# A three-layer graph network on one core: layer 1's last four spans taken from running sums of gathered rows

## The chip, the cores and the metric

The kernel runs on one core of a Trainium2 chip. Its engines are TensorE (PE, with its weight loads shown as PEld), VectorE (DVE), ScalarE (ACT), GpSimd (POOL) and SyncE (SP, which here only starts DMAs). The metric is the device time of one execution in microseconds (us), less being better; a kernel's time is the median of its runs.

## The reference, cut to what matters

There are 6,250 nodes with 128 features and 200,000 edges, sorted by target node (`dst`). Three GRU layers with edge weights are followed by a layer norm, then by three GIN layers without weights and a second norm:

```python
for l in range(3):                              # GRU layers
    msg = (x @ weight[l])[src] * edge_weight[:, None]
    agg = segment_sum(msg, dst, num_segments=6250)
    x = gru_cell(agg, x, w_ih, w_hh, b_ih, b_hh)
x = layernorm(x0 + x)
for W, b in ((W0, b0), (W1, b1), (W2, b2)):     # GIN layers
    x = relu((x + segment_sum(x[src], dst)) @ W.T + b)
out = layernorm(x1 + x)
```

## The kernel before, in words

**Aggregation as dense matrices.** The node states lie as `xT`, feature by node, and node-major as `Y`, 49 tiles of 128 nodes. An aggregation is a matmul of all 49 tiles of Y with a strip of the adjacency matrix for some target nodes. Two matrices are needed: `adj_w` with the summed edge weights (float32, GRU layers) and `adj_h` with the edge counts (float16, GIN layers). Both are built during GRU layer 1 and stored in DRAM.

**Layer 1: 28 slots.** The target nodes are cut into 28 spans of 224 nodes, and slot t builds span t. Each node owns 64 places for edges, and two nodes share the 128 partitions. A slot has 8 batches of 14 node pairs ("windows"). For each batch DVE makes two comparisons, `hot` (which of the 49 tiles does each edge's source lie in, L2129, 700 elements) and `hot_lo` (which row of the tile, L2131, 1,792 elements), and three products of `hot` with the weights, which are split into three bfloat16 parts (L2135, 700 elements each). PE's `build_unit` (L1232) multiplies them: for each window and half, one matmul of 98 columns (counts and first weight part) and two of 49 (the other parts), 84 in a batch. ACT moves the sums out of PSUM in 6 evictions a batch (L1653), three for counts and three for weights, and SP stores the finished strips (`store_strips`).

While slot t is built, PE aggregates the span of slot t - 1 between the batches (`add_tiles`, L1239: 49 tiles of 224 columns, float32, two passes each) and runs the GRU gates of the span of slot t - 2 (`fused_rz`, `fused_ih`, L1252 to L1259), with sigmoids and tanh on ACT (L1618, L1623) and `fused_mix` and `fused_blend` on DVE (L2096 to L2110). POOL fetches the next spans' edges with indirect DMAs (`gather`, L775; `gather_near`, L757) and writes each edge's key, row and weight parts as columns that DVE's comparisons read (`make_columns`, L796 to L802). DVE's slot t + 1 waits for these columns. PE unrolls slots 0 and 1 and runs slots 2 to 27 in a loop over one slot's body. DVE waits for `s_keep`, the store of `xT` to `x_keep`, before that loop.

**Runs in layers 2 and 3.** The last 4 spans' aggregates are not made from `adj_w` there. The last 128 x 224 edges are cut into 128 lanes of 224 consecutive edges. In round i POOL gathers the source rows of the i-th edge of every lane (`fetch_rows`, L858), DVE multiplies them by the weights (L1816) and adds the sum so far if the target node is the same (L1819). Every running sum is stored in `sum_rows`. A node's aggregate is the sum at its last edge, plus that of the lane before if its edges cross a border: POOL gathers both (`fetch_ends`, L872), DVE adds them (`join_ends`) and PE turns them (`flip_runs`). The strips of `adj_w` for these spans are aggregated in layer 1 but not stored.

**The order** is written out by hand on every engine: each waits for counts of semaphores, such as `s_bmm` (units built), `s_bev` (evicted), `s_hot` (comparisons and products), `s_colv` (column steps), `s_acc` (rounds summed) and `s_fgv` (gate steps).

## Time and profile before

| | |
|---|---|
| median of 3 runs | 2909.53 us (2908.0 to 2910.0) |
| the profiled execution's own time | 2905.17 us |
| its span | 2903.3 us |
| PE busy | 2842.1 us, 98% |
| DVE, ACT, POOL busy | 1290.2, 947.2, 815.7 us |
| layer 1, slots 3 to 27 | 142.5 to 1003.4 us |

The span goes from the first to the last instruction; the execution's own time is 1.9 us longer. Busy time is summed by engine; PE's matmuls are pipelined, and their ends are modelled, so the start of one group to the start of the next gives PE's price better than the durations.

### The profile page before, as it was taken

What the parts mean: (1) busy time and instruction counts of PE and PEld (TensorE: products, weight loads), DVE (VectorE), ACT (ScalarE), POOL (GpSimd) and SP (SyncE); (2) the same over time, 40 slices, a digit from 0 to 9 for tenths busy, and PEclk for the clock granted to TensorE, in tenths of its full rate; (3) what the DMA queues carried; (4) which work ended last, traced back from release to release, by engine and by line L of the source; (5) the groups of instructions that cost most, each with busy time, mean ns of one, the idle gap of its engine ahead of it and who ended that gap; (6) DMA issues with size and microseconds to landing.
All of it is one profiled execution on the core that took longest, in us unless ns stands there. A gap on an engine that the chain in (4) does not pass through costs nothing.

```text
span 2903.3 us, 72862 instructions
## 1 busy us (share of the span) xinstructions
PE 2842.1 (98%) x29387; PEld 1888.8 (65%) x29387; DVE 1290.2 (44%) x3163; ACT 947.2 (33%) x1891; POOL 815.7 (28%) x977
## 2 busy tenths in 40 slices
PE   5899999999999999999999999999999999999998
PEld 5899999999999965555554555555555555555554
DVE  7688888888888614344422344343400010001111
ACT  6677777777777610000001011101300010001111
POOL 4233333333333215454531445543100000000000
PEclk9999999999999999999999999999999999999999
DMA  5666666666662299988996888988478768786884
GB/s 195 241 260 261 244 242 260 259 256 241 249 258 115 94 404 345 341 338 331 353 364 233 340 338 331 362 325 328 152 304 301 300 257 306 300 301 255 311 304 166
DMA packets 134137, 810.64 MB, mean 279 GB/s; under 512 B 17208, under 2 KB 27308, under 8 KB 114076
## 3 DMA queue, kind: packets, MB, share of 16 engines
q1 hardware_dynamic: 111516, 759.24, 67.5%
q0 software_dynamic: 19808, 39.54, 4.3%
q10 hardware_dynamic: 2720, 10.62, 0.9%
q8 instruction: 57, 0.93, 0.1%
q14 instruction: 36, 0.29, 0.0%
HBM read 553.01 MB, written 256.33 MB: 279 GB/s over the span
## 4 chain that ended last, share of the span: by engine, by line
PE 95%; DVE 1%; ACT 1%; another core or an unknown queue 1%; issue 1%; DMA 1%; POOL 0%; DVEq 0%; ACTq 0%; POOLq 0%
PE ps L961 30%; PE ps L1157 27%; PE ps L1239 19%; PE ps L1232 11%; PE ps L971 1%; PE ps L972 1%; PE ps L1252 1%; PE ps L1253 1%; PE ps L974 1%; PE ps L973 1%; PE ps L1136 1%; ACT ring L1653 0%; DMA x_keep<-xT 0%; PE ps L1258 0%
## 5 line engine op out<-in xcount | busy, mean ns | idle before, releaser
L961 PE MATMUL ps<-ring,Y 128*128 128x448 f32 x2352 | 888.4, 539 | 0.0
L1157 PE MATMUL ps<-ring,Y 128*128 128x448 f16 x4116 | 780.6, 352 | 0.0
L1653 ACT ACTIVATE ring<-ps 128x490 f16<-128x490 f32 (+1 forms) x1344 | 699.1, 656 | 188.6 <-PE ps L1232 184.4
L961 PEld LDWEIGHTS ps<-ring,Y 128*128 128x128 f32 x2352 | 446.4, 190 | 434.8 <-issue 434.8
L1157 PEld LDWEIGHTS ps<-ring,Y 128*128 128x128 f16 x4116 | 402.7, 98 | 373.8
L858 POOL DMA_INDIRECT ring<-y_rows,ring x448 | 430.5, 961 | 519.1 <-PE ps L961 261.3
L1239 PE MATMUL ps<-ring,Y 128*128 (+1 forms) x2744 | 571.8, 360 | 0.4 <-ACT shared L1612 0.4
L1239 PEld LDWEIGHTS ps<-ring,Y 128*128 128x128 f32 x2744 | 504.9, 190 | 8.9 <-ACT shared L1612 0.8
L1232 PEld LDWEIGHTS ps<-shared 64*128 64x128 bf16 x18816 | 325.8, 94 | 84.7 <-issue 67.0
L1232 PE MATMUL ps<-shared 64*128 64x49 bf16 (+1 forms) x18816 | 351.8, 190 | 25.3 <-DVE shared L2135 14.6
L2135 DVE TENSOR_TENSOR shared<-shared 128x700 bf16<-128x700 bf16 x672 | 324.8, 538 | 0.0
L1816 DVE TENSOR_SCALAR ring<-ring 128x128 f32<-128x128 f32 x446 | 129.9, 291 | 388.0 <-DMA ring<-y_rows,ring 224.8
L2131 DVE TENSOR_TENSOR shared<-iota_lo,shared 128x1792 bf16<-128x1792 bf16 x224 | 253.7, 1132 | 0.0
L1560 ACT ACTIVATE xT<-ps,bcur,unscale 128x448 f32 (+1 forms) x42 | 30.4, 723 | 682.1 <-PE ps L1157 682.1
L1392 ACT ACTIVATE shared<-ps 128x448 f32<-128x448 f32 x24 | 13.0, 543 | 725.5 <-PE ps L961 684.0
L1999 DVE TENSOR_REDUCE x_tops<-xT x28 | 17.4, 620 | 482.3 <-ACT xT L1560 482.3
L2129 DVE TENSOR_TENSOR shared<-iota_key,shared 128x700 bf16<-128x700 bf16 x224 | 119.9, 535 | 151.9 <-PE ps L1232 136.0
L1819 DVE SCALAR_TENSOR_TENSOR ring<-ring 128x128 f32<-128x128 f32 x446 | 157.0, 352 | 47.6 <-DVE ring L1816 0.9
L775 POOL DMA_INDIRECT shared<-in_edges,take_now x60 | 93.5, 1559 | 265.6 <-PE ps L1232 262.3
L1965 DVE TENSOR_TENSOR shared<-shared,ps 128x384 f32 (+3 forms) x14 | 8.7, 621 | 228.5 <-PE ps L1172 228.1
L732 POOL COPY weights_stage<-shared 112x128 f32<-112x128 f32 x28 | 17.9, 639 | 189.1 <-DVE shared L2058 189.1
L1733 DVE SCALAR_TENSOR_TENSOR shared<-ps,bhh,shared 128x448 f32<-128x448 f32 x28 | 19.1, 683 | 91.6 <-ACT shared L1409 81.5
(195 smaller groups left out, 1418.0 us busy)
## 6 DMA issues: line engine op xcount, KB each, us to landing
ring<-adj_w SPq DMA_DIRECT2D x72, 2688.0 KB
ring<-adj_h SPq DMA_DIRECT2D x42, 2800.0 KB, 9.5
ring<-adj_h SPq DMA_DIRECT2D x42, 2688.0 KB, 9.2
adj_w<-ring SPq DMA_DIRECT2D x48, 2016.0 KB, 11.9
adj_h<-ring SPq DMA_DIRECT2D x56, 1372.0 KB, 5.4
ring<-adj_w SPq DMA_DIRECT2D x24, 2912.0 KB
adj_w<-ring SPq DMA_DIRECT2D x48, 728.0 KB, 6.8
sum_rows<-ring SPq DMA_DIRECT2D x64, 448.0 KB
```

The costliest lines, as they stand in the source:

```text
L775: pool.indirect_dma_start(out=edges_now[:, par, d * SHARE:d * SHARE + OWN, :].bitcast(I32) .rearrange("p e k -> p (e k)"), out_offset=None ...
L858: pool.indirect_dma_start(out=run_rows[:, i % ROW_BUFS, :], out_offset=None, in_=y_rows, in_offset=bass.IndirectOffsetOnAxis(ap=run_edges[ ...
L961: mm = pe.matmul(ps[:, bank, 0:GW], Y[:, h, :], slab(s)[:, :, h - h0, :], start=(h == 0), stop=(last and h == TILES - 1))
L1157: mm = pe.matmul(ps[:, par, 0:GW], part[:, h, :], counts_slab(par, s)[:, :, h - h0, :], start=(h == 0 and part is Y_high), stop=(h == TILE ...
L1232: mm = pe.matmul(sums, hot_lo[slots, buf, w, :], rhs, start=(part == 0), stop=(part == WPARTS - 1))
L1239: mm = pe.matmul(ps[:, AGG_BANK, 0:SPAN], Y[:, h, :], strip_w[:, bass.ds(slot, 1), :, h, :].rearrange("p o b c -> p (o b) c"), start=(h == ...
L1653: act.activation(strip[:, :, c0:c0 + UNIT * WIN].rearrange("p h (d j) -> p d h j", d=WIN)[:, :, :, w0:w1], psum_unit(a)[:, :, kind, :, :]. ...
L1816: dve.tensor_scalar(run_rows[:, buf, :], run_rows[:, buf, :], weight, None, ALU.mult).then_inc(s_prod, 1)
L1819: dve.scalar_tensor_tensor(out=run_sums[:, at, :], in0=run_sums[:, (i - 1) % SUM_BUFS, :], scalar=same_node, in1=run_rows[:, buf, :], op0= ...
L2129: dve.tensor_tensor(in_pairs(hot[:, buf, :, 0, :]), every_window(iota_key, WIDE), values(par, 0, k, WIDE), ALU.is_equal).then_inc(s_hot, 1)
L2131: dve.tensor_tensor(in_pairs(hot_lo[:, buf, :, :]), every_window(iota_lo, P), values(par, 1, k, P), ALU.is_equal).then_inc(s_hot, 1)
L2135: dve.tensor_tensor(in_pairs(hot[:, buf, :, 1 + part, :]), in_pairs(hot[:, buf, :, 0, :]), values(par, 2 + part, k, WIDE), ALU.mult).then_ ...
```

## The change

- Layer 1 takes the last 4 spans from running sums too. Their 224 rounds gather rows of the input `x` itself: 2 rounds in each of the first 7 batches of 16 slots (1 to 3, 6 to 8, 11 to 13, 16 to 18, 21 to 24). POOL gathers (`fetch_batch`), ACT scales a batch later (`scale_rows`), DVE sums four batches later (`sum_batch`), SP stores after five, four rows at a time.
- The build slots come in a new order: four times four dense spans and one of the last four spans ("stretches" of five slots), then the other eight dense spans. The slots of the last four spans (4, 9, 14, 19) build counts alone: no products, 28 matmuls of 49 columns a batch, 3 evictions.
- The tiles of the dense span in front of such a slot are added half in it (24 tiles) and half in the slot behind it (25 tiles), which runs no gates. Four sets of gates thereby go to the tail behind slot 27, with `flip_run` for the four run spans; the order of the gates is `GATE_ORDER`.
- The three weight products become one instruction of 2,100 elements; `hot` and `columns` get other layouts for it, and the columns are made in 7 steps instead of 6.
- The rounds use 16 buffers, summed in place, where there were 10 for rows and 14 for sums. This holds for layers 2 and 3 too.
- DVE waits for `s_keep` at its first blend instead of ahead of the loop. `run_edges` is loaded by SP at the start. PE loops three times over a body of five slots and unrolls the rest; the other engines unroll all slots. The scratch for POOL's DMAs is set to 8192 bytes.

```diff
-ROW_BUFS = 10
-STORE = 7
+RUN_BUFS = 16
+STORE = 4
...
+FIRST_RUN = GATHERS - RUN_SPANS
+STRETCH_DENSE = 4
+STRETCH = STRETCH_DENSE + 1
+STRETCHED = RUN_SPANS * STRETCH
+ORDER = [span for r in range(RUN_SPANS) for span in (*range(STRETCH_DENSE * r, STRETCH_DENSE * (r + 1)), FIRST_RUN + r)]
+ORDER += range(STRETCH_DENSE * RUN_SPANS, FIRST_RUN)
+GATE_ORDER = [*range(FIRST_RUN - 1), *range(FIRST_RUN, GATHERS), FIRST_RUN - 1]
+RUN_SLOTS = [1, 2, 3, 6, 7, 8, 11, 12, 13, 16, 17, 18, 21, 22, 23, 24]
+RUN_BATCHES = 7
+SCALE_LAG, SUM_LAG, STORE_LAG = 1, 4, 5
+HALF_ADDED = 24
+TAIL_TILES = [0, 6, 15, 24, 33, 42, TILES]
...
+        def rounds_at(n):
+            slot, k = divmod(n, BATCHES)
+            if n < 0 or slot not in RUN_SLOTS or k >= RUN_BATCHES:
+                return range(0)
+            first = RUN_PER_BATCH * (RUN_BATCHES * RUN_SLOTS.index(slot) + k)
+            return range(first, first + RUN_PER_BATCH)
...
+            def fetch_round(turn, i):
+                if i >= RUN_BUFS:
+                    if i % STORE == 0:
+                        use, q = divmod(i // STORE - STORE_TURNS, STORE_TURNS)
+                        pool.wait_ge(s_stored[q], 16 * (STORES // STORE_TURNS * turn + use + 1))
+                    pool.wait_ge(s_acc, RUN * turn + i - RUN_BUFS + 2)
+                pool.indirect_dma_start(out=run_bufs[:, i % RUN_BUFS, :], out_offset=None, in_=y_rows if turn else x,
+                                        in_offset=bass.IndirectOffsetOnAxis(ap=run_edges[:, i, 0:1].bitcast(I32), axis=0))\
+                    .then_inc(s_row[i % RUN_BUFS], 16)
...
+            def prepare_span(t):
+                par = t % 2
+                n = BATCHES * t
+                for k in range(2):
+                    fetch_batch(n + k)
+
+                pool.wait_ge(s_key, OWN_TILES + KEY_STEPS * (t + 2))
+                pool.wait_ge(s_colp, t + 1)
+                pool.sem_inc(s_mark_pool, 1)
+                add_own(t + 1, 1 - par)
+                take_places(t + 2, par)
+                if t in (ENDS_SLOT, ENDS_SLOT + 1):
+                    first = RUN_SPANS // 2 * (t - ENDS_SLOT)
+                    fetch_ends(0, range(first, first + RUN_SPANS // 2))
+                fetch_batch(n + 2)
+                for d, k in enumerate(FETCH_AT):
+                    pool.wait_ge(s_bmm, UNITS * (BUFS + n + k))
+                    pool.sem_inc(s_mark_pool, 1)
+                    gather(par, d)
+                    fetch_batch(n + k)
+                    if d == 0:
+                        fetch_batch(n + k + 1)
+                make_columns(t + 1, 1 - par)
+                fetch_batch(n + 6)
+                near_rows(t + 3, 1 - par)
...
-            def build_unit(n, buf, a):
+            def build_unit(buf, a, weighted):
...
-                    for part in range(WPARTS):
+                    for part in range(WPARTS if weighted else 1):
...
+                    tiles = range(0 if j else HALF_ADDED, TILES if weighted else HALF_ADDED)
...
-            with pe.Fori(0, GATHERS // 2 - 1) as i:
-                with pe.Fori(0, 2) as slot:
-                    build_span(2 * i + slot + 2, slot, 2 * i + slot)
...
+            for j in range(2, STRETCH):
+                build_span(0, j)
+            with pe.Fori(1, RUN_SPANS) as r:
+                for j in range(STRETCH):
+                    build_span(r, j)
+            for j in range(GATHERS - STRETCHED):
+                build_span(RUN_SPANS, j)
...
-            add_tiles(0, 0, SH)
-            fused_gates(GATHERS - 2)
...
+            for c, n in enumerate(range(FIRST_RUN - 2, GATHERS)):
+                add_tiles(0, TAIL_TILES[c], TAIL_TILES[c + 1])
+                if n < GATHERS - 1:
+                    fused_gates(n)
...
+                if c < RUN_SPANS:
+                    flip_run(c)
...
+            def scale_rows(n):
+                for i in rounds_at(n):
+                    row = run_bufs[:, i % RUN_BUFS, :]
+                    act.wait_ge(s_row[i % RUN_BUFS], 16 * (i // RUN_BUFS + 1))
+                    act.activation(row, row, ACT.Copy, scale=run_edges[:, i, 1:2]).then_inc(s_prod if i else s_acc, 1)
...
+            def sum_row(turn, i):
+                done = RUN * turn + i
+                row, last = (run_bufs[:, j % RUN_BUFS, :] for j in (i, i - 1))
+                dve.wait_ge(s_acc, done)
+                dve.wait_ge(s_prod, done - turn)
+                dve.scalar_tensor_tensor(out=row, in0=last, scalar=run_edges[:, i, 2:3], in1=row,
+                                         op0=ALU.mult, op1=ALU.add).then_inc(s_acc, 1)
...
-                    dve.wait_ge(s_hot, HOT * n + 1)
-                    for part in range(WPARTS):
-                        dve.tensor_tensor(in_pairs(hot[:, buf, :, 1 + part, :]), in_pairs(hot[:, buf, :, 0, :]),
-                                          values(par, 2 + part, k, WIDE), ALU.mult).then_inc(s_hot, 1)
+                    if has_weights(t):
+                        dve.wait_ge(s_hot, hot_before(t, k) + 1)
+                        dve.tensor_tensor(hot[:, buf, 1:KINDS, :, :].rearrange("p k w (x t) -> p (k w) x t", t=2),
+                                          hot[:, buf, 0:1, :, :].rearrange("p k w x -> p k (w x)").to_broadcast([P, WPARTS, BATCH * WIDE]),
+                                          columns[:, par, k, 2:2 + WPARTS, :, :].rearrange("p k w (o t) -> p (k w) o t", o=1)
+                                          .to_broadcast([P, WPARTS * BATCH, WIDE // 2, 2]), ALU.mult).then_inc(s_hot, 1)
+                    sum_batch(n - SUM_LAG)
...
-            dve.wait_ge(s_keep, 16)
...
+                if n == 0:
+                    dve.wait_ge(s_keep, 16)
```

## Rows read from the trace of the kernel before

**Rows 1.** Page, the span in 40 slices, busy tenths of PE
```profile
PE   5899999999999999999999999999999999999998
```
**Rows 2.** Stretches: length, busy time by engine (instructions), PE clock, DMA share, GB/s
```profile
0.00:104.00 104.00, 67.34 (x1567) 58.76 (x1569) 68.27 (x153) 62.61 (x124) 36.38 (x75) 0.93 0.66 239
...
142.50:1003.40 860.90, 860.72 (x19626) 798.97 (x19625) 716.75 (x1469) 662.30 (x1325) 306.19 (x404) 1.00 0.58 230
1003.40:1030.50 27.10, 26.65 (x155) 26.16 (x155) 3.20 (x9) 5.32 (x13) 0.89 (x2) 1.00 0.73 303
```
**Rows 3.** Stretches: one slot (columns: PE, PEld, DVE, ACT, POOL, clock, DMA)
```profile
486.76:521.18 34.42, 34.42 (x786) 31.95 (x785) 28.89 (x60) 26.50 (x53) 12.07 (x16) 1.00 0.63 253
```
**Rows 4.** Timeline of PE in that slot: start, duration, line
```profile
488.23 0.65 PE L1252 MATMUL ps<-shared,wT 128*128 128x224 f32 x2
...
489.95 1.53 PE L1232 MATMUL ps<-shared 64*128 64x98 bf16 x84
491.41 2.92 PE L1239 MATMUL ps<-ring,Y 128*128 x14
494.16 0.54 PE L1258 MATMUL ps<-shared,wT 128*128 128x224 f32 x2
...
495.01 0.66 PE L1232 MATMUL ps<-shared 64*128 64x98 bf16 x30
```
**Rows 5.** Timeline of DVE in slot 0, one batch and the next one's start
```profile
23.80 0.53 DVE L2129 TENSOR_TENSOR shared<-iota_key,shared 128x700 bf16<-128x700 bf16 x1
...
25.24 1.38 DVE L2135 TENSOR_TENSOR shared<-shared 128x700 bf16<-128x700 bf16 x3
26.54 0.52 DVE L2129 TENSOR_TENSOR shared<-iota_key,shared 128x700 bf16<-128x700 bf16 x1
```
**Rows 6.** Waits from 0 to 150 us: total, times, longest
```profile
PE ps L1232 <- DVE shared L2135: 14.6, 3, 7.4
...
DVE shared L2129 <- DMA x_keep<-xT: 12.2, 1, 12.2
```
**Rows 7.** Stretches: the time after that wait
```profile
99.60:106.40 6.80, 3.74 (x88) 3.57 (x89) 6.40 (x16) 2.69 (x6) 0.00 (x0) 0.50 1.00 415
```
**Rows 8.** Groups and one line's instructions: nearest rows for gate steps, sums, scalings
```profile
L2099 DVE SCALAR_TENSOR_TENSOR shared<-ps,bih,shared 128x224 f32<-128x224 f32 x12 | 5.4, 451 | 0.4
...
L1819 DVE SCALAR_TENSOR_TENSOR ring<-ring 128x128 f32<-128x128 f32 x446 | 157.0, 352 | 47.6 <-DVE ring L1816 0.9
...
L1570 ACT ACTIVATE shared<-shared,averager x47: 477/480/494, 2688.3 to 2898.7; - x35, 128x128 f32<-128x128 f32 x12
```
**Rows 9.** Row gathers of layers 2 and 3: all (ns min/median/max), then the timeline
```profile
L858 POOL DMA_INDIRECT ring<-y_rows,ring x448: 938/944/1252, 1068.5 to 2008.1; - x150
...
1259.25 0.94 POOL L858 DMA_INDIRECT ring<-y_rows,ring  x1 [0.30 <-DVE ring L1819]
```
**Rows 10.** Timeline of POOL at the start and in one slot; DVE's next slot begins
```profile
13.98 1.01 POOL L775 DMA_INDIRECT shared<-in_edges,take_now  x1 [0.84 <-POOL take_now L769]
...
497.40 1.69 POOL L775 DMA_INDIRECT shared<-in_edges,take_now  x1 [2.66 <-PE ps L1232]
506.01 1.54 POOL L775 DMA_INDIRECT shared<-in_edges,take_now  x1 [6.92 <-PE ps L1232]
...
512.72 0.44 POOL L800 CAST shared<-shared 128x224 bf16<-128x224 f32 x1 [0.17 <-POOL shared L802]
...
518.45 0.52 DVE L2129 TENSOR_TENSOR shared<-iota_key,shared 128x700 bf16<-128x700 bf16 x1 [1.48 <-PE ps L1232]
```
**Rows 11.** Timeline of PE where it stops inside a unit (slots 1 and 2)
```profile
68.84 0.71 PE L1232 MATMUL ps<-shared 64*128 64x49 bf16 x33 [0.85 <-issue]
...
129.19 0.29 PE L1232 MATMUL ps<-shared 64*128 64x49 bf16 x7 [1.99 <-issue]
```
**Rows 12.** DMA queues of instructions, 0 to 142.5 us, then 142.5 to 1003.4 us (packets, MB, share)
```profile
q8 instruction: 18, 0.29, 0.8%
...
q14 instruction: 4, 0.03, 0.0%
```

531 lines of the change are left out of this document (291 added, 240 removed).

## The prediction

> **What bounds the kernel now.** I read the page's slices first, then busy time by stage, then one slot of the layer-1 stage engine by engine. TensorE (PE) is busy in almost every slice [rows 1]. The change works in the first 1030 us. From 142.5 to 1003.4 us (slots 3 to 27, 34.4 us each) PE is busy 860.7 of 860.9 us, so there a gain is what leaves PE, as long as nobody else becomes the bound [rows 2]. One slot shows how near the others are: PE 34.4, DVE 28.9, ACT 26.5, POOL 12.1 us [rows 3]. PE's prices come from its timeline [rows 4]: one batch's build 1.46 us (489.95 to 491.41), seven aggregated tiles 2.75 to the gates behind them (0.40 a tile), gates 1.72 (r, z: 488.23 to 489.95) and 0.85 (494.16 to 495.01). DVE takes 2.74 us a batch (23.80 to 26.54), 1.44 of it the two comparisons, to the products at 25.24 [rows 5]; what is left of its 28.9 is 7.0 a slot for keys, steps, leaps and gates.
>
> **The stall in front of slot 2.** DVE waits 12.2 us there for the store of x, and PE 7.4 us in one piece for DVE [rows 6]; PE's granted clock then falls to 0.50 for 6.8 us, the lower level of 1.2 GHz [rows 7], in which its 3.7 us of work would be 1.9. The wait on s_keep moves from ahead of the loop to the first blend, some 20 us into slot 2. **-9.**
>
> **Four counts-only slots and the slots behind them.** A counts slot (j = 4) builds with a third of the matmuls. No row shows that batch; a third of 1.46 is 0.49, and in no case is it above 1.46. With 24 tiles, gates, and transposes (0.5, what is left of the slot's 34.4) PE has 3.9 + 9.6 + 2.6 + 0.5 = 16.6 us. DVE has 8 x 1.44 + 7.0 + six left-over sums at 0.39 = 20.9, ACT half its evictions, about 14.3. So DVE ends it, and POOL's columns for the next slot may add half a microsecond: 21.5. The slot behind (j = 0) has a full build but 25 tiles and no gates: PE 11.7 + 10.0 + 0.5 = 22.2, ACT 24.9 (its slot without gates), DVE 8 x 2.62 + 7.0 - 2.1 (five gate operations of up to 0.45 us, [rows 8]) = 25.9. Together 47.4 instead of 68.8; DVE comes in up to 4.5 us ahead of PE and must leave with 2.6 done, which gives another 0 to 2. I take 22 for each of four pairs: **-88** (bounds -76 and -96).
>
> **Merged product.** Three products of 700 elements stand in the 1.38 us row; one of 2,100 saves the overlapping starts, 0.12 us. It is off PE's path except at j = 0, where it is in the sum. Were it to run at half the element rate it would cost some 2.3 us, see the rivals.
>
> **Tail.** From 1003.4 PE runs 27.1 us to layer 2: 49 tiles, two sets of gates, turned chunks [rows 2]. Four more sets come in (4 x 2.57 = 10.3) and four flips (1.2); these gates were left out of the j = 0 slots above. One set's chain (r, z 1.72, then seven operations of DVE and ACT at up to 0.45 as in [rows 8], with hand-overs some 6) is shorter than PE's turn of 2.57 + 0.5 + nine tiles 3.6 = 6.7, so only its first and last ends show: **+13** (up to +18 if a joined row is late).
>
> **The run rounds, on four engines.** 224 rounds go into 16 slots, 14 a slot, all inside PE-bound slots. DVE gets 14 sums of 352 ns [rows 8], 0.39 with the dependent wait, less 8 x 0.12: 28.9 + 5.5 - 1.0 = 33.4. ACT gets 14 scalings; the nearest row is L1570, the same shape at 480 ns, 0.41 in a row [rows 8]: 26.5 + 5.7 = 32.2. Both stay under 34.4, by one to two microseconds, and DVE may run a batch ahead, so a late row is caught up rather than passed on. POOL is another matter. It is busy 12.1; three gathers that start 0.9 us after what releases them (PE ends a batch at 495.01 + 1.46, the gather starts at 497.40), seven dependent steps 0.17 apart and one more column step, 0.5, make 16.5, say 17 [rows 4, 10]. Fourteen gathers come on top. In layer 2 one costs 938 to 944 ns and they follow each other every 1.25 us [rows 9]. In the build stage the edge gathers take 1.69 and 1.54 us where one took 1.01 at the start of the kernel: each of these began while DVE was in its comparisons [rows 10]. So 14 gathers are 17.5 us from below and 14 x 2.0 = 28 from above. Only those that meet a comparison or the product should be lengthened, so I take 1.5 each, 21 us, and POOL's slot is 38. Against a PE slot of 35.8 (next part) that is 2.2 late a slot. In the first slot of each of four groups it is covered, since columns were ready 5.3 us before DVE used them (512.72 + 0.44 against 518.45, [rows 10]); in the other 12 it is not: **+27** (0 to +126). Queued behind a late gather are make_columns, for which DVE's next slot waits, and ACT's scaling, behind which stand the evictions.
>
> **PE's code.** This is what I would have missed without asking what stood in front of idle PE. In slots 1 and 2 PE stops inside a unit, with nothing to wait for: 0.85 us at 68.8 and 1.99 us at 129.2 [rows 11]. Instruction transfers of 16 KB go with it: 18 of them before 142.5 us, and in the 861 us of the loop none on that queue [rows 12]. So PE stalls where it meets code for the first time while the DMA engines are full of strip stores, and a one-slot loop body stays resident. The new PE code unrolls slots 0 to 4, loops over a body of five slots three times, and unrolls eight more. 11 PE-bound slots with new code are certain; if the five-slot body doesn't stay, it is 17. I take 17 at the 1.4 us a slot that slots 1 and 2 show, four j = 0 slots at the same, and two jumps back at 2.5: 24 + 6 + 5 = **+35**. Bounds: 11 slots at 1.4, +15; each of a slot's two store bursts catching one full stall, 4 us, 17 x 4 + 16 + 5 = +89.
>
> The Trainium skill (Runtime: NRT & Kernel Launch, section Instruction fetch mechanics) says that PE's instruction memory holds 2048 instructions, is refilled in blocks of 256, and that crossing a block is mostly hidden. The first half agrees with 16 KB packets and with a resident loop; the trace disagrees with the second by 1.99 us in one crossing. By that rule the stalls would be nought and the sum 35 lower. The same section says that a taken branch to code no longer held forces a fetch, which speaks for the two jumps.
>
> **Small ones.** The first columns in one more step, place_ends (18 dependent steps) on DVE in slot 25, eight end gathers on POOL in each of slots 26 and 27: **+3** together. Seven more iotas on POOL at the start end before the first leap count arrives. Loading run_edges moves x by 1 to 2 us, ahead of its first use. In layers 2 and 3 the stores are 56 of 4 rows instead of 32 of 7 and the rows share 16 buffers; PE there waited for none of it. 0.
>
> **Sum.** -9 - 88 + 13 + 27 + 35 + 3 = -19, against the profiled execution's 2905.2 (span 2903.3), which is 4.3 below the median of the runs, 2909.5. So 2886 in its terms and **2891** in those of the median.
>
> **Rivals.**
> 1. *Code fetch costs nothing* (the page's rule, as a mechanism here: blocks arrive ahead as they seem to in layers 2 and 3, where a block lasts long). 2891 - 35 = 2856; if gathers too keep their quiet price of 1.25, POOL's slot is 34.5 and 27 more go: 2829. Against it stand two stalls in two slots.
> 2. *POOL becomes the bound of the run slots.* At 2.0 us a gather its slot is 45, 9.2 above PE's: 16 x 9.2 less 4 x 5.3 is +126 in place of +27, so 2990, slower than before. It decides from 1.6 us a gather, where 12 x 1.6 us eats the 19 gained. For it: each of the edge gathers in the build stage is at 1.54 or above. Against: these always start right at a batch's end, as DVE starts comparing; fourteen in a row will not.
> 3. *Code fetch is dear*, 4 us a slot: +54, 2945, slower. For it: the DMA engines are nearly as busy in the loop, 0.58, as in the first 104 us, 0.66 [rows 2], and strip stores recur in every slot.
> 4. *The merged product loses its rate*: DVE's run slots at 33.4 + 8 x 1.0 = 41.4, over 5 us above PE in every full slot, about +120, so 3010. Its operands keep pairs of 16-bit elements, as before.
> 5. *The work is taken out but nobody waits less*: not likely, as PE is the bound without a gap.
>
> **Chances.** Forecast 0.43, between 2865 and 2903; rival 1 0.22; rival 2 0.14; rival 3 0.14; rival 4 0.03; rest 0.04 (any of them cut down to nearly no change). Under 0.2% (5.8 us) a measurement of this kernel can't be told from no change. From these: faster 0.58, same 0.12, slower 0.30. The range takes in rival 1's first value and the full price of rival 3, and leaves out the far ends: 2842 to 2950.
>
> **What the next profile would show.** PE's slots from 142 us on no longer alike: pairs of about 21 and 26 us, the others 34.4 plus stalls. L1232's batches in counts slots near 0.5 us. Waits of PE on "issue" of some tens in number and 25 to 40 us in sum, with instruction packets in the whole of the first 900 us (some 150 more) if the body isn't resident. Gathers on POOL in layer 1 at 1.2 us each and their line's idle small; if they are at 1.6 or more, or DVE's first comparison of a slot and ACT's scaling wait for POOL or its DMA by tens of microseconds, rival 2 is the case. No 12 us wait for x_keep. PE idle in the tail of a few microseconds. What would make me wrong outright: DVE rather than PE last in the run slots, a merged product above 1.5 us, or a lower clock in the counts slots, where PE has gaps.

## The result and the profile after

The changed kernel takes **26,368.9 us** (median of 4 runs, 26,355.2 to 26,374.5), before took 2908.8 us beside it: ratio 9.07, interval 9.057 to 9.079. I had forecast 2891 us and faster. Three single executions far above their neighbours (3001.5 and 10,422.0 us of before, 8803.6 us of one layout) are left out of the times below. The page of after shows at once that this is no slower layer 1 but another program. Its slices of the 26,372.7 us span (0.66 ms each, tenths of busy time, then granted clock and GB/s):

```profile
PE   8500000000000000000000000000000000399999
DVE  7403333333333333333333333333333333200000
POOL 5303333333333333333333333333333333100000
PEclk9755555555555555555555555555555555699999
GB/s 248 299 338 15 15 15 15 15 15 15 15 15 15 15 15 15 15 15 15 15 15 15 15 15 15 15 15 15 15 15 15 15 15 15 129 260 263 253 292 254
```

For some 21 ms TensorE does nothing and 15 GB/s move. The groups between 1082 and 23,000 us say who works there:

```profile
L979 POOL DMA_INDIRECT adj_w<-w_sum,cell x1600 | 3185.7, 1991 | 14920.0 <-DVE cell L2390 12481.1 <-issue 2438.9
L979 POOL DMA_INDIRECT adj_c<-count,cell x1600 | 3181.0, 1988 | 487.8 <-issue 487.8
```

1600 turns of two scattered adds are the kernel's other branch: it builds the adjacency in blocks of 125 edges and then runs all three layers densely. Every engine takes it when `flag` is 0, and `flag` is 1 only if the counted sum is N_EDGES + RUN_SPANS*SPAN. The second part of that sum is a test of L2312, which counts the starts of the four counts-only spans that are at least RUN_BASE (171,328). Two places in VectorE's timeline of after show what reaches it (start, duration, line):

```profile
917.51 0.16 DVE L1914 SCALAR_TENSOR_TENSOR run_last<-run_from,found 112x8 f32<-112x8 f32 x1
917.71 0.31 DVE L1916 TENSOR_SCALAR run_from<-run_from 112x8 f32<-112x8 f32 x1
...
1033.97 0.15 DVE L2312 TENSOR_SCALAR_CACHE_REDUCE run_mask<-run_from 112x8 f32<-112x8 f32 x1
...
1050.29 0.15 DVE L2315 TENSOR_SCALAR flag<-ps 1x1 int32<-1x1 f32 x1 [16.17 <-PE ps L1454]
```

L1916 is the step of `place_ends` that subtracts RUN_BASE from `run_from` in place. It used to run in layer 2, behind the test; it now runs in slot 25, 116 us ahead of it. The test then compares starts that have already lost 171,328 with 171,328.

Layer 1 of this trace is still the changed layer 1. Its tail begins (first tiles behind the last slot) at 1045.28 us, against 1003.4 in [rows 2]. The stretches of after, columns as in [rows 2]:

```profile
0.00:104.00 104.00, 67.27 (x1602) 58.98 (x1602) 75.31 (x145) 65.66 (x136) 58.71 (x100) 0.85 0.67 237
104.00:980.00 876.00, 767.35 (x16815) 691.48 (x16816) 688.91 (x1229) 654.27 (x1392) 532.75 (x630) 0.95 0.65 251
980.00:1045.30 65.30, 58.77 (x1282) 53.61 (x1280) 40.26 (x65) 43.46 (x86) 34.14 (x40) 0.97 0.60 216
```

TensorE is busy 893.4 us up to the tail (67.3 + 767.4 + 58.8), where before it was 964.6. So 71 us of work did leave it, and its idle time rose from 39 to 152 us: +42 in all. The waits of TensorE from 104 to 980 us name the idle time (total, times, longest):

```profile
PE ps L1318 <- issue: 59.8, 35, 4.2
PE ps L1318 <- DVE shared L2269: 20.3, 6, 4.9
PE ps L1318 <- ACT ring L1781: 9.5, 12, 1.7
PE ps L1325 <- issue: 8.4, 8, 2.6
PE ps L1351 <- ACT shared L1727: 6.8, 4, 6.3
```

"issue" with nothing to wait for, 68 us, is the largest. In before PE had 0.2 us idle in 861 [rows 2], and its granted clock was 1.00 there; here it is 0.95.

### The profile page after: what moved, and what is told of

The parts are those of the page before. It is cut to its first block, busy times and chain, and to the rows that moved or that the text cites. A ratio compares the mean times of both kernels' runs of the same rounds, so it can differ in the third digit from the quotient of the medians.

```text
span 26372.7 us, 202033 instructions
## 1 busy us (share of the span) xinstructions
PE 4401.5 (17%) x29364; PEld 2609.4 (10%) x29364; DVE 9180.1 (35%) x49850; ACT 927.1 (4%) x1904; POOL 6992.3 (27%) x3969
## 4 chain that ended last, share of the span: by engine, by line
DVE 28%; issue 27%; DMA 23%; PE 16%; SPq 3%; POOL 3%; DVEq 0%; POOLq 0%; ACT 0%; ACTq 0%
DMA adj_c<-count,cell 22%; PE ps L1045 12%; SPq L719 3%; POOL adj_w L979 2%; DVE shared L2355 2%; DVE shared L2354 2%; PE ps L1325 1%; DVE part_i L2387 1%; DVE scal L2383 1%; DVE scal L2386 1%; DVE scal L2366 1%; DVE scal L2373 1%; DVE cell L2390 1%; DVE scal L2379 1%; DVE scal L2377 1%
## 5 line engine op out<-in xcount | busy, mean ns | idle before, releaser
L979 POOL DMA_INDIRECT adj_w<-w_sum,cell x1600 | 3185.7, 1991 | 14920.0 <-DVE cell L2390 12481.1
L1014 PE MATMUL ps<-ident,xT 128*128 128x128 f32 x147 | 28.8, 346 | 21756.1 <-DMA shared<-x_keep 21743.9
L979 POOL DMA_INDIRECT adj_c<-count,cell x1600 | 3181.0, 1988 | 487.8 <-issue 487.8
L1045 PE MATMUL ps<-ring,Y 128*128 128x448 f32 x8232 | 3107.6, 539 | 6.5 <-DVE Y L1855 6.5
L1045 PEld LDWEIGHTS ps<-ring,Y 128*128 128x128 f32 x8232 | 1563.3, 190 | 1536.9 <-issue 1536.9
L2358 DVE CUSTOM_DVE_ANT_0 shared<-shared 125x125 f32<-125x125 f32 x3200 | 927.5, 290 | 110.5
L2355 DVE SCALAR_TENSOR_TENSOR shared<-shared,dst_c 125x125 f32<-125x125 int32 x1600 | 561.5, 351 | 57.3
L1325 PE MATMUL ps<-ring,Y 128*128 128x224 f32 x2352 | 526.2, 376 | 9.1 <-issue 8.7
L2358 DVE CUSTOM_DVE_ANT_0 shared<-shared,earlier 125x125 f32<-125x125 f32 x1600 | 463.5, 290 | 55.5
L2364 DVE TENSOR_SCALAR_CACHE_REDUCE shared<-thresholds,scal 125x55 f32<-125x55 f32 x1600 | 434.7, 272 | 56.9
L2371 DVE TENSOR_SCALAR_CACHE_REDUCE shared<-thresholds,scal 125x55 f32<-125x55 f32 x1600 | 434.3, 271 | 56.9
L1325 PEld LDWEIGHTS ps<-ring,Y 128*128 128x128 f32 x2352 | 450.3, 199 | 22.4 <-issue 8.9
L2383 DVE TENSOR_SCALAR scal<-scal 125x1 f32<-125x1 f32 x1600 | 342.2, 214 | 56.9
L2386 DVE TENSOR_SCALAR scal<-scal 125x1 f32<-125x1 f32 x1600 | 341.6, 214 | 57.3
```

The source lines that it names most:

```text
L979: pool.indirect_dma_start(out=adj.rearrange("(e o) -> e o", o=1), out_offset=bass.IndirectOffsetOnAxis(ap=cell[:, 0:1], axis=0), in_=val[: ...
L1045: mm = pe.matmul(ps[:, bank, 0:GW], Y[:, h, :], slab(s)[:, :, h - h0, :], start=(h == 0), stop=(last and h == TILES - 1))
L1325: mm = pe.matmul(ps[:, AGG_BANK, 0:SPAN], Y[:, h, :], strip_w[:, strip, :, h, :], start=(h == 0), stop=(h == TILES - 1))
L2355: step(dve.scalar_tensor_tensor(out=both, in0=dst_r[:, :], scalar=dst_c[:, 0:1], in1=same, op0=ALU.is_equal, op1=ALU.mult))
L2358: step(dve.tensor_tensor_reduce(junk, both, other[:, :], 1.0, 0.0, ALU.mult, ALU.add, acc[:, :]))
L2383: step(dve.tensor_scalar(m1, major, float(ROW), keep, ALU.mult, ALU.mult))
```

## Experiments

### The branch

One constant of the changed kernel is altered, so that the test suits starts that already had RUN_BASE taken off:

```
-            dve.tensor_scalar(run_mask[:, :, :], run_from[:, :, :], float(RUN_BASE), 0.0, ALU.is_ge, ALU.add,
+            dve.tensor_scalar(run_mask[:, :, :], run_from[:, :, :], 0.0, 0.0, ALU.is_ge, ALU.add,
                               accum_out=covered[:, 1:2]).then_inc(s_found, 1)
```

> The changed kernel with one constant altered: the coverage test counts the starts of the four counts-only spans that are at or above 0 instead of at or above 171,328. Nothing is left out; the instructions and their order are those of the changed kernel. Theory A (the placing of the run ends now runs ahead of the test and has already taken 171,328 off the starts, so that the test finds none, the flag is 0 and every engine takes the other branch): the flag is 1, the branch of before is taken, and the time is that of before plus what layer 1 lost in the trace of after, where its tail starts at 1045 us against 1003 us before, plus up to 15 us for the longer tail: 2950 to 2965 us. Theory B (the flag is 0 for another reason, the sum of the found edges): nothing changes, about 26,370 us. Theory C (the branch is taken as before, and the added time is the new layer 1 and its consequences): about 26,370 us as well.

3022.6 us (3018.9 to 3028.9, 5 runs), ratio to before 1.040 (1.038 to 1.041). Theory A stands for the 23.3 ms: theories B and C said 26,370. But my number was 60 us short, and that is the second story of this case.

The other way round, before with a flag that must fail (it is compared with `N_EDGES + RUN_SPANS*SPAN - 1`, and GpSimd waits for two early copies in the other branch):

> The kernel before with the flag compared with a number one less than the one that the counted sum reaches, so that the flag is 0 and the other branch is taken (GpSimd waits there once for two early copies into sum_rows, over long before); layer 1 is built as before. Theory A (the branch alone makes the time of after): the time of after less the 42 us that its layer 1 took longer, 26,300 us within 1%. Rival (something in the changed layer 1 slows the later stages too): well under 26,000 us.

26,319.4 us, one run. Beside it the changed kernel itself took 26,428.6, 109 us more, and its tail of layer 1 began 104 us later (1106.46 against 1002.57 us). So the old layer 1 with the other branch costs what the changed kernel costs, less what layer 1 lost. The branch alone makes the 23 ms.

### Why the mended kernel is 115 us slower

The trace of the altered test has its tail of layer 1 at 1111.24 us, 66 us behind the trace of the changed kernel, with the same instructions. TensorE and GpSimd around 264 us in it (timeline; brackets: idle before, releaser):

```profile
262.88 0.89 PE L1318 MATMUL ps<-shared 64*128 64x98 bf16 x44
264.05 0.28 PE L1318 MATMUL ps<-shared 64*128 64x49 bf16 x5 [0.28 <-issue]
264.80 0.74 PE L1318 MATMUL ps<-shared 64*128 64x98 bf16 x35 [0.48 <-issue]
265.47 2.92 PE L1325 MATMUL ps<-ring,Y 128*128 128x224 f32 x14
```
```profile
262.10 0.95 POOL L890 DMA_INDIRECT run_bufs<-in_x,run_edges  x1 [0.30 <-issue]
263.36 0.94 POOL L890 DMA_INDIRECT run_bufs<-in_x,run_edges  x1 [0.30 <-issue]
```

A batch of 84 build matmuls, 1.46 us when undisturbed, is cut up by gaps of 0.25 to 0.5 us with a handful of matmuls between them. From 100 to 1000 us I counted gaps of TensorE with releaser issue ("short gaps"): here 179 of up to 0.6 us, over half of them beginning while a row gather runs, though gathers fill only a quarter of that time; in the trace of the changed kernel 7. Kernels timed together on one chip are called a sitting here; there were six, and the altered test and the changed kernel's first trace come from two of them. Two runs asked whether the gaps belong to the program or to the sitting.

> The changed kernel once more, nothing altered. In its trace the tail of layer 1 (the first multiply of L1325 that waits 0.45 us for L1727) starts at 1045 us; in the changed kernel with the altered test, whose layer 1 has the same instructions in the same order, it starts at 1111 us, with 200 more gaps of 0.25 to 0.5 us between build matmuls (releaser issue), half of them while GpSimd issues L890's row gathers. If these gaps belong to the run or the chip and not to the program, this run and the next agree with each other, at 1045 us or at 1111 us. If they belong to the program, this one has its tail at 1045 us again and the next at 1111 us. The time is about 26,370 us either way.

> The changed kernel with the altered test once more (starts counted from 0), nothing left out. If the gaps belong to the program: 3015 to 3030 us with the tail of layer 1 at about 1111 us and over 150 short gaps. If they belong to the run or the chip: anything between 2950 us with the tail at 1045 us and 3025 us.

The changed kernel again: 26,428.6 us, tail at 1106.46 us, 177 short gaps. The altered test again: 3018.0 us, tail at 1102.79 us, 177 short gaps. So the program alone doesn't decide: the same kernel shows 7 in one trace and 177 in another.

In the same sitting, the 224 row gathers are taken out (GpSimd only signals; products, sums and stores go on with zeros; edit shortened):

```
 def fetch_round(turn, i):
     ...
+    if not turn:
+        pool.sem_inc(s_gone, 1); return
     pool.indirect_dma_start(out=run_bufs[:, i % RUN_BUFS, :], ...)
```

> The changed kernel with the altered test, and without the 224 gathers of rows of x (L890, turn 0): GpSimd only signals where it issued one, run_bufs is cleared once at the start instead, and the products, sums, stores and end gathers of the rounds go on with zeros, so that four spans of layer 1 get no sums. Theory G (GpSimd's row gathers hold back TensorE's matmuls: 98 of the 175 short gaps lie under one): the short gaps go, and the time falls by 60 to 90 us, to 2930 to 2960 us. Rival H (the gaps have to do with the instructions of TensorE alone): 10 us less at most, 3010 to 3020 us, the gaps still there. Rival I (DVE's 223 sums of 0.36 us and ScalarE's 224 products set the pace, not the gathers): the time stays within 10 us too, and no gap of releaser issue changes.

2924.9 us (ratio 1.007, 1.006 to 1.009), 27 short gaps, tail at 1007.98 us. Theory G: the gathers, not the 223 sums or the 224 products, cost some 93 us there (the tail begins 95 us earlier). What in them? Plain copies of 128 neighbouring rows, same place, same bytes (edit shortened):

```
+    if not turn:
+        pool.dma_start(run_bufs[:, i % RUN_BUFS, :], x[128 * (i % 44):128 * (i % 44) + 128, :]); return
```

> The changed kernel with the altered test, where each of the 224 gathers of rows of x (L890, turn 0) is a plain copy of 128 rows that lie together in x, issued from the same place on GpSimd: the same bytes into the same buffers in the same rhythm, but the rows are not those that the edges name, so four spans get wrong sums. Without these gathers the time was 2925 us, with them 3019 to 3023 us. Theory G1 (it is the making of 128 row addresses and descriptors on GpSimd, 0.94 us per gather, that holds TensorE back): the short gaps of 0.25 to 0.5 us between build matmuls are few, as in the run without gathers (25 instead of 175), and the time is 2925 to 2950 us. Rival G2 (it is the traffic of the rows, 128 packets of 512 bytes each, wherever it comes from): over 100 short gaps, 3000 to 3025 us. Rival G3 (a plain copy on GpSimd's queue costs it as much as a gather): GpSimd's busy time per copy is again 0.9 us and more, and the gaps stay.

2934.7 us and 13 short gaps; but the next kernel of that sitting, with its gathers, had 7, so the run told nothing of them. It was repeated, with the altered test beside it:

> Once more the kernel in which each of the 224 gathers of rows of x is a plain copy of 128 rows that lie together, issued by GpSimd (four spans get wrong sums). Its first run stood on a chip on which the layout with the last seven slots in a loop took 2915 us and had no short gaps either, so it told nothing of them. If the run beside this one (the changed kernel with the altered test) shows over 150 short gaps: G1 (the making of the rows' descriptors holds TensorE back) gives 2925 to 2950 us and few gaps here; G2 (the rows' traffic does) gives 3000 to 3025 us and over 100. If the run beside it shows few gaps and about 2955 us, this one gives 2925 to 2945 us and tells nothing of them again.

> The changed kernel with the altered test, nothing left out, on the same chip as the plain copies: 3015 to 3030 us with over 150 short gaps, as in its three runs so far, or, if this is the kind of chip of the first trace of the changed kernel, 2950 to 2965 us with few.

Altered test 3033.5 us, 176 short gaps; plain copies 2952.1 us (ratio 1.015, 1.013 to 1.017), 25 short gaps. GpSimd's row for the copies from 0 to 1000 us (in the first of the two runs), and for the gathers in the next kernel:

```profile
L892 POOL DMA_DIRECT2D run_bufs<-in_x x224 | 123.3, 557 | 125.6 <-PE ps L1322 99.0 <-DMA sum_rows<-run_bufs 8.9 <-POOL shared L865 7.1
```
```profile
L890 POOL DMA_INDIRECT run_bufs<-in_x,run_edges x224 | 251.6, 1123 | 98.5 <-issue 56.0 <-PE ps L1318 20.1 <-POOL take_now L834 10.5
```

G2 and G3 fall: where the gaps occur, they go with the plain copies, though GpSimd's DMA queue moves no less (from 100 to 860 us 18.4 MB in 9,317 packets, with the gathers 16.7 MB in 8,460), and a copy takes GpSimd 0.56 us instead of 1.12. G1 is what is left, its forecast of 2950 missed by 2 us. But a gather differs from the copy in two ways that no run separates: GpSimd makes a list from 128 row numbers, and the rows lie scattered in DRAM.

The clearest look at the effect is slot 26 of a layout in which the last seven slots are one loop body (its runs follow below). There eight gathers of run ends stand back to back. Without short gaps in the sitting the slot took 34.1 us, with them 45.3, with not one packet of TensorE's instructions on queue q8 in either: this isn't code being fetched. With the gaps TensorE got through 2 to 6 matmuls at a time, and over the slot its granted clock was 0.89 (PE, POOL, then the slot's stretch):

```profile
1003.95 1.05 PE L1318 MATMUL ps<-shared 64*128 64x98 bf16 x49
1005.45 0.29 PE L1318 MATMUL ps<-shared 64*128 64x98 bf16 x6 [0.46 <-issue]
1006.21 0.32 PE L1318 MATMUL ps<-shared 64*128 64x98 bf16 x6 [0.47 <-issue]
...
1009.88 0.32 PE L1318 MATMUL ps<-shared 64*128 64x98 bf16 x5 [1.18 <-issue]
1011.35 0.31 PE L1318 MATMUL ps<-shared 64*128 64x98 bf16 x4 [1.15 <-issue]
```
```profile
1004.17 1.00 POOL L903 DMA_INDIRECT run_bufs<-sum_rows,run_ends  x1 [1.08 <-issue]
1005.47 0.93 POOL L903 DMA_INDIRECT run_bufs<-sum_rows,run_ends  x1 [0.30 <-issue]
```
```profile
995.80:1041.10 45.30, 38.80 (x788) 34.26 (x789) 27.37 (x45) 26.57 (x53) 21.93 (x25) 0.89 0.54 203
```

It also fits that the kernel before is free of the gaps (1 in the trace with the failing flag, in the sitting where both kernels with row gathers had 177): in that trace, as in [rows 10], its 50 edge gathers from 142.5 to 1000 us start behind a finished batch, and none lies over build matmuls. Of the row gathers of the layout above, 136 of 197 do.

### TensorE's code

The kernel before, with only TensorE's slot loop written out (edit shortened):

```
-with pe.Fori(0, GATHERS // 2 - 1) as i:
-    with pe.Fori(0, 2) as slot:
-        build_span(2 * i + slot + 2, slot, 2 * i + slot)
+for t in range(2, GATHERS):
+    build_span(t, t % 2, t - 2)
```

> The kernel before with TensorE's loop over slots 2 to 27 written out, 26 copies of the body for one; every instruction of the work, every wait and every other engine stay as they are. Theory of code fetch (TensorE's instructions that it has not executed lately come in by transfers that queue behind the strip stores): the trace of after has 76 us of waits with the releaser issue on the build's matmuls in layer 1, in 26 slots of new code, 16 of which only; here all 26 are new: 2909 plus 60 to 80, 2970 to 2990 us. Rival (new code costs nothing, the issue gaps of after come from elsewhere, such as the merged product or the counts-only matmuls): 2905 to 2915 us. The 1.4 us per slot of the prediction would give 2945 us.

2974.3 us, ratio 1.023 (1.021 to 1.024): +67 us for 26 slots of new code, 2.6 us a slot, and the rival (2905 to 2915) falls. From 0 to 1060 us TensorE's waits on issue are 45.0 us ahead of build matmuls and 7.2 ahead of others, against 6.2 in before:

```profile
PE ps L1232 <- issue: 45.0, 31, 3.0
```

Part of the rest is the clock behind a stall. TensorE in the trace of the altered test, where 14 tiles behind a stall take 5.49 instead of 2.92 us at a granted clock of 0.51:

```profile
1068.50 0.77 PE L1318 MATMUL ps<-shared 64*128 64x49 bf16 x22 [2.76 <-issue]
1069.20 5.49 PE L1325 MATMUL ps<-ring,Y 128*128 128x224 f32 x14
```

In the written-out kernel the granted clock over 142.5 to 1072 us is 0.99 where [rows 2] has 1.00.

The same in the mended kernel: can the stalls be taken back with loops? First, slots 1 to 3 of a stretch and the last seven slots as loops (edit shortened):

```
 with pe.Fori(1, RUN_SPANS) as r:
-    for j in range(STRETCH): build_span(r, j)
-for j in range(GATHERS - STRETCHED): build_span(RUN_SPANS, j)
+    build_span(r, 0)
+    with pe.Fori(1, STRETCH_DENSE) as j: build_span(r, j)
+    build_span(r, STRETCH_DENSE)
+build_span(RUN_SPANS, 0)
+with pe.Fori(1, GATHERS - STRETCHED) as j: build_span(RUN_SPANS, j)
```

> The changed kernel with the altered test, and with TensorE's code in loops: the slots 1 to 3 of a stretch of five are one body run three times (stretches 1 to 3), and the last seven slots are one body run seven times, so that some 1500 instructions stay in use instead of some 9000. Nothing is left out. Theory of code fetch: most of the 76 us of issue waits of layer 1 go, and the time is 50 to 70 us below the changed kernel with the altered test: 2885 to 2910 us. Rival (the issue waits only stand where TensorE would wait for VectorE or ScalarE anyway, whose busy share of the layer is 0.79 and 0.75): within 15 us of the changed kernel with the altered test.

3058.3 us, 36 us slower than without the loops: both of my theories failed. I had also counted badly, matmuls without weight loads: one weighted slot's body is some 1600 instructions of TensorE, and three kinds of slot did not stay together. Most jumps back of the short loops show as a pair of stalls, 2.0 to 2.6 and 5.2 to 6.0 us, and as many instruction packets move as before (35 from 300 to 500 us, against 31). Then only the last seven slots as a loop and the stretches written out, `for r in range(1, RUN_SPANS)`:

> The changed kernel with the altered test, with TensorE's code laid out in another way: the four stretches of five slots are written out one after another (no loop over them, so no branch back), and the last seven slots are one body run seven times. Nothing is left out. In the run with loops in every stretch each branch back cost two stalls, of 2.0 and 5.6 to 6.0 us, and in the changed kernel the branch back of the loop over stretches cost 5.8 and 2.7 us, twice; the last slots, run from one body, had no stall of releaser issue over 0.6 us outside the slots of the end gathers. Theory: 17 us less for the two branches and 1.5 to 2.5 us for each of six repeated slots, 2990 to 3000 us. Rival (stalls of TensorE's code are hidden or made up for by the waits after them): within 5 us of 3018 to 3023 us.

2915.1 us (ratio 1.0033, 1.0017 to 1.0048), far below what I expected, in a sitting without the short gaps. Whether layout or sitting did it, four kernels in one sitting were to tell:

> The changed kernel with the altered test, nothing left out, once more, now on one chip with the layout that took 2915 us. Program theory P (the 200 short gaps come from the loop over stretches, which brings TensorE's code in again and again while GpSimd gathers rows): 3015 to 3030 us, tail of layer 1 at 1103 to 1111 us, over 150 short gaps; the written-out layouts beside it have under 40. Chip theory Q (the gaps depend on the chip or the loading of the program, as the two traces of the changed kernel itself show, tail at 1045 and at 1106 us): all kernels of this call that gather rows agree, with gaps in all or in none; without them this one takes 2945 to 2965 us.

> Stretches written out, last seven slots one body run seven times (the layout that took 2915 us), nothing left out. P: 2907 to 2925 us again, under 40 short gaps. Q with the gaps on this chip: 2980 to 3000 us; Q without them: 2907 to 2925 us, and the changed kernel with the altered test beside it is 30 to 45 us slower, the price of two branches back and of six slots' new code.

> The changed kernel with the altered test and TensorE's code of all 28 slots written out, no loop at all, nothing left out. P: few short gaps, and only the stalls of new code in every slot, so 15 to 25 us above the layout with the last seven slots in a loop: 2930 to 2945 us. If the loop of the last seven slots is what matters: as the changed kernel with the altered test.

> As the layout with the last seven slots in a loop, and in each of the stretches 1 to 3, written out, slots 1 to 3 are one body run three times (its waits counted from one register only, as in the last seven slots, where the repeats had no stall over 0.6 us). Nothing is left out. Theory (a body that is run again from TensorE's instruction memory has no stalls): six slots fewer of new code at 1.9 us each, 10 to 15 us less than the layout with the last seven slots in a loop. Rival (a body of about one slot run three times is fetched anew each time, as in the run with both loops, where 35 instruction packets moved between 300 and 500 us, no fewer than the 31 of the changed kernel with the altered test, and each branch back cost 2.0 and 5.6 to 6.0 us): 30 to 50 us more.

| layout of TensorE's code | us, one sitting | short gaps | tail of layer 1 at |
|---|---|---|---|
| as the change has it (loop over stretches) | 3027.0 (ratio 1.041) | 166 | 1111 |
| last seven slots one loop | 3007.1 (1.034) | 179 | 1087 |
| all written out | 3012.7 (1.037) | 178 | 1094 |
| also slots 1 to 3 of a stretch a loop | 3033.4 (1.042) | 146 | 1122 |

The same kernel (second row) took 2915 us in one sitting and 3007 in this one, and the written-out layouts have the gaps too: theory P falls. In each sitting with several kernels that gather rows, all have the gaps or none has, as Q says. But the chip's number alone doesn't decide either: chip 13 was used in two sittings, with 7 gaps in the one (second row's kernel) and 176 in the other (altered test). The layout is worth 20 us here.

Do loops keep the code? Count the instruction packets of 16 KB on queue q8 [rows 12] slot by slot. The last seven slots as a loop fetch 6 in their first pass and none in the next six, in all four traces of such a loop. The three-fold loop of the fourth layout behaves in two ways: in slots 6 to 8 and 16 to 18 it fetches 8 or 9 packets in every slot, more than the 6 of written-out code, and stands still behind a jump, as in this row; in slots 11 to 13 it fetches 6, 0 and 0. The body and the number of passes are the same, only its place in the code differs; what about the place decides it is not shown. In the first version of the short loops (3058.3 us) all nine slots fetched 8 or 9. The fourth layout came out 26 us above the second: the rival's direction, a little under its 30 to 50.

```profile
296.87 1.34 PE L1318 MATMUL ps<-shared 64*128 64x98 bf16 x42 [5.90 <-issue]
```

The quiet run of the second layout (2915.1 us) is the best look at the change with few gaps and its last slots' code resident. Its stretches, one slot each, are slots 14 (counts only), 15, 23 (with rounds), 25 and 26 (without), columns as in [rows 3], then TensorE in slot 14:

```profile
525.80:547.20 21.40, 17.33 (x288) 14.44 (x288) 18.11 (x34) 14.83 (x30) 12.34 (x16) 1.00 0.82 326
547.20:576.10 28.90, 25.82 (x727) 22.87 (x729) 26.43 (x41) 24.29 (x48) 14.27 (x18) 0.88 0.48 189
819.00:855.80 36.80, 34.60 (x787) 31.86 (x787) 30.84 (x57) 30.16 (x68) 26.74 (x32) 1.00 0.73 283
894.50:929.40 34.90, 34.41 (x787) 31.75 (x789) 31.58 (x53) 26.14 (x52) 15.03 (x18) 1.00 0.66 259
929.40:963.50 34.10, 34.10 (x786) 31.69 (x785) 28.07 (x45) 26.48 (x53) 22.16 (x25) 1.00 0.72 269
```
```profile
538.23 0.53 PE L1318 MATMUL ps<-shared 64*128 64x49 bf16 x28
538.69 1.78 PE L1325 MATMUL ps<-ring,Y 128*128 128x224 f32 x8
541.29 0.53 PE L1318 MATMUL ps<-shared 64*128 64x49 bf16 x28 [0.83 <-DVE shared L2272]
```

Slots 22 to 24 have rounds and no code stall, and they take 37.5 us on average, 3.0 more than before. Their waits (781.9 to 894.5 us) name the chain: ACT waits for a gathered row to land, and TensorE for ACT's eviction behind it.

```profile
ACT run_bufs L1751 <- DMA run_bufs<-in_x,run_edges: 19.2, 12, 4.1
...
PE ps L1318 <- ACT ring L1784: 5.9, 6, 2.0
DVE shared L2270 <- POOL shared L865: 4.8, 2, 2.7
```

Layer 1 up to its tail, from the start of one group of slots on TensorE to the start of the next, in us:

| | before | quiet layout | changed kernel, first trace |
|---|---|---|---|
| slots 0 to 2 | 142.6 | 140.6 | 142.5 |
| four pairs (counts-only slot and the one behind) | 275.4 | 212.3 | 220.2 |
| the 14 slots with rounds from slot 3 on | 482.2 | 541.5 | 564.4 |
| slots 25 and 26 | 68.8 | 69.1 | 76.4 |
| slot 27, to the tail | 34.9 | 34.8 | 41.8 |
| start of the tail | 1003.9 | 998.3 | 1045.3 |

VectorE at the two slot starts behind slot 14:

```profile
544.43 0.53 DVE L2270 TENSOR_TENSOR shared<-iota_key,shared 128x700 bf16<-128x700 bf16 x1 [1.36 <-POOL shared L865]
...
555.48 0.52 DVE L2270 TENSOR_TENSOR shared<-iota_key,shared 128x700 bf16<-128x700 bf16 x1
555.92 1.08 DVE L2272 TENSOR_TENSOR shared<-iota_lo,shared 128x1792 bf16<-128x1792 bf16 x1
556.92 1.25 DVE L2276 TENSOR_TENSOR shared<-shared 128x2100 bf16<-128x2100 bf16 x1
558.08 0.52 DVE L2270 TENSOR_TENSOR shared<-iota_key,shared 128x700 bf16<-128x700 bf16 x1
...
571.97 0.53 DVE L2270 TENSOR_TENSOR shared<-iota_key,shared 128x700 bf16<-128x700 bf16 x1 [1.95 <-POOL shared L865]
```

### Single parts of the change in the kernel before

The wait for x_keep alone moved to the first blend:

```
-            dve.wait_ge(s_keep, 16)          # ahead of slot 2
 def fused_blend(n):
+                dve.wait_ge(s_keep, 16)
```

> The kernel before with one part of the change alone: VectorE's wait for the copy of the input states (L1612's neighbour, x_keep) stands ahead of the first write to these states, in the first blend, and not ahead of the third slot. The trace of before shows 12.2 us of VectorE waiting there and 7.4 us of TensorE behind it. The prediction's term: 9 us less, 2896 to 2901 us. Rival (the copy then runs beside the slot and the slot waits for something else, such as the strips' stores, just as long): 2904 to 2908 us.

2903.1 us, ratio 0.9981 (0.9972 to 0.9990). The wait for x_keep is gone, TensorE's wait for the products falls from 14.6 to 7.7 us:

```profile
PE ps L1232 <- issue: 8.7, 5, 3.2
...
PE ps L1232 <- DVE shared L2136: 7.7, 2, 5.8
PE ps L1214 <- DVE shared L2066: 5.9, 1, 5.9
```

but 2.7 us more of code stall and 2.1 more ahead of the transposes come back (6.0 and 3.8 in before over the same 300 us): -4.9 instead of -9. It is the one version here that measured below before, by 0.2%.

> The kernel before with one part of the change alone: the space in SBUF for the descriptors of GpSimd's gathers is 8192 bytes of each partition, as in the changed kernel. In before GpSimd issues its 448 row gathers in 0.96 us each in the later layers and 60 gathers of edges in layer 1. Theory (nothing waits for this space): 2904 to 2910 us, gathers at 0.96 us. Rival (half the space makes a gather wait for the ones ahead of it): gathers take over 1.1 us, and the time rises by 5 us or more.

2908.6 us, ratio 1.000 (0.999 to 1.001), gathers at 0.94 us: with `dynamic_dma_scratch_size=8192` alone nothing is lost. This sitting had no short gaps, so whether the smaller space matters where they occur is not shown.

## Why the prediction was wrong

**The step that failed** is "place_ends (18 dependent steps) on DVE in slot 25", which I put under small ones at +3 with the first columns and the end gathers. I costed its duration and not its order. It writes `run_from`, and a test that decides the branch reads `run_from` later. The two timeline rows, the altered test (3022.6) and the failing flag in before (26,319.4) show it from both sides. The prediction has no rival in which the program takes its other branch. Nothing in the trace of before could show it; the diff does, in the two places where `place_ends()` is called.

**Without that step I would still have been wrong in sign.** The altered test is 1.040 times before, and even from the quiet trace the mended kernel comes to about 1045.3 + 1915.8 = 2961 (the tail of after's trace, and what the altered test took from its tail to its end), an estimate, against 2903.3. Term by term:

- *Stall at slot 2, -9.* The mechanism was right, the size measured -4.9.
- *Counts-only slot and the slot behind, -88.* The prices were right: the counts batch takes 0.53 us (0.49 was worked out), VectorE's batch 2.60 (2.62: 555.48 to 558.08), slot 14 21.4 (21.5; the other three counts-only slots 22.2 to 26.6). But the four pairs gained 63 us in the quiet layout and 55 in the changed kernel. The slot behind takes 28.8 us instead of 25.9 (slot 15): 3.9 us of code stalls, which the prediction counted elsewhere, then a granted clock of 0.88, and 1.36 of VectorE's wait for GpSimd's columns, where I had allowed 0.5. GpSimd makes the columns behind the second edge gather, and in slots this short VectorE is through first. A wait of 1.6 us for a landing gather of nodes, inside slot 14, I didn't have at all.
- *Merged product, off the path.* Right: 1.25 us each, rival 4 is dead.
- *Tail, +13.* Right: from the same tile group to layer 2 TensorE took 26.6 us before, 37.5 in the altered test and the quiet layout, +11. To the end of the program it is +14 to +16, so what comes behind the tail took 3.5 to 5.5 us for which I had 0.
- *Run rounds, +27.* Too low, with the weight on the wrong one of its two paths and a third path missing. Where gaps are few, 3.0 us in each of slots 22 to 24 make some 48 for 16 slots, an estimate. GpSimd is not the bound (26.7 us busy of 36.8, gathers at 1.12 on average, far from the 1.6 at which rival 2 decides). What holds TensorE is ACT's scaling, which waits for a row to land with the evictions behind it. Late columns are the smaller part. And where short gaps occur, the gathers hold TensorE back directly: 81 us against plain copies, 93 against no gathers (which holds their quiet price too), 92 for the second layout between two sittings. That path the prediction didn't have: it treated GpSimd as a station in a queue.
- *TensorE's code, +35.* The cause was right, the size half: 68 us of issue waits in the changed kernel, and +67 for 26 slots in before, 2.6 us a slot where I took 1.4 from two stalls. That is nearer to rival 3 (89 in place of 35, with 4 us on 21 slots). The rule of the Trainium skill (Runtime: NRT & Kernel Launch, section Instruction fetch mechanics) that crossing a block is mostly hidden doesn't hold in this stage: 35 waits of up to 4.2 us ahead of build matmuls. Its other rule, that a taken branch whose target isn't in the current two-page window forces a fetch, agrees with the stalls of 5.2 to 6.0 us behind jumps back; but before jumps back over some 1600 instructions, more than two blocks of 256, with no packet on q8 from 142.5 to 1003.4 us, and there the trace decides.
- *Small ones:* the descriptor space 0, as forecast.

So up to the tail I forecast -32. The changed kernel's first trace has +41: 55 gained in the pairs, and 82 lost in the 14 slots with rounds (some 42 for the rounds by the 3.0 us above, an estimate, the rest code) and 15 in the last three slots, whose code is new too. The quiet layout has -6, the one trace with the new slots in which layer 1 came out shorter than before. With gaps the same layout's tail begins 88 us later, the changed kernel's 61.

**Open.** What tells a sitting with short gaps from one without is not found: neither the program alone nor the chip's number alone does, and where a program's code and buffers come to lie when it is loaded was not looked at. Why gathers hold back TensorE's matmuls, by making the list or by the scattered rows, wasn't separated either. Gaps under other GpSimd steps (L861, L797) were there too, fewer. The gaps and the code stalls also trade: in the second layout the stalls of over 0.6 us from 100 to 1000 us fell from 51 to 21 us when the gaps came.

## What to carry to other kernels

When a change moves a step, list what the step writes and who reads it in the new order, before any price; a guard that picks a branch deserves the first look, since its price isn't a term of the sum but the whole other program. Count code as a resource of TensorE: a body that stays in its instruction memory ran 861 us with 0.2 us idle, each new slot of it cost 2.6 us, and a short loop over a long body was refetched in two places and stayed in a third, so count instruction packets slot by slot before a loop is trusted. And time a kernel in more than one sitting before a layout is praised: 2915 and 3007 us were one program.

## What the hardware showed that I hadn't expected

- Row gathers from GpSimd's list (0.95 us each) cut a run of dense small matmuls into pieces: 146 to 179 gaps of mostly 0.25 to 0.5 us in 900 us in four of six sittings, 7 in the other two; 25 to 27 with plain copies or without gathers.
- The matmuls of 224 columns (L1325) show nearly none of these gaps, those of 49 and 98 columns (L1318) nearly all.
- One loop body of a slot, run three times, fetched 8 or 9 packets in every slot in one stretch, with stalls of up to 5.9 us, and 6, 0 and 0 in the next. Run seven times, slot 26 takes 34.1 us, as in before.
